# Reordering the work in front of a fused kernel's tile loop, and three small moves inside the loop

## The reference, cut to what matters

```python
# x: (64, 64, 1024), float32; W is L0_ffn_weight (1024, 1024)
y = grouped_conv(x, L0_cond_weight, K=9, groups=4) + (cond_128 @ c_weight.T)[:, :, None] + bias
w_scale = max(abs(W), axis=-1) / 127;  w_q = round(W / w_scale)          # int8, per row
a_scale = max(abs(y), axis=-1) / 127;  y_q = round(y / a_scale)          # int8, per token
x = x + float16((y_q @ w_q.T) * a_scale * w_scale.T)
# second layer, float32
h = gelu(gelu(cond_128 @ W0 + b0) @ W1 + b1);  att = softmax(h @ W2 + b2)
u = einsum('boi,bih->boh', einsum('bk,koi->boi', att, weight), x) + (att @ bias_k)[:, :, None]
H = u @ W2nd.T + b;  z = u @ A
gate = top-2 softmax gate of H[:, odd tokens, :8] and z[:, odd tokens] @ LiMEs.T, scaled by their global maxima
x = x + H + ((z * (gate @ LiMEs)) @ Bmat) * 0.5
```

## Time and profile before

| | |
|---|---|
| median of 3 runs | 624.28 us (623.23 to 624.49) |
| the profiled execution | 624.99 us |
| its span, first to last instruction | 623.2 us |
| PE busy | 612.7 us (98%) |
| DVE, ACT, POOL busy | 423.5, 348.1, 374.2 us |
| mean granted TensorE clock | 0.999 |

### The profile page before, as it was taken

One profiled execution on the slowest core, in us unless ns is written; L12 is line 12 of the kernel. 1 busy time (PEld: TensorE's weight loads), 2 busy tenths in 40 slices (PEclk: granted clock), 3 DMA queues, 4 the chain that ended last, 5 costly groups with the idle time before them and its releaser, 6 DMA issues.

```text
span 623.2 us, 15758 instructions
## 1 busy us (share of the span) xinstructions
PE 612.7 (98%) x6297; PEld 343.4 (55%) x6297; DVE 423.5 (68%) x845; ACT 348.1 (56%) x614; POOL 374.2 (60%) x252
## 2 busy tenths in 40 slices
PE   8999999999999999999999999999999999999997
PEld 6756666666666776666454444444444444444443
DVE  5868888977888888887688976664535444345534
ACT  2878999778988888875652442545153332233000
POOL 3316554547766666546596948798967656865300
PEclk9999999999999999999999999999999999999999
DMA  8968998888888988774056105855455344544203
GB/s 346 334 192 281 390 303 281 277 301 296 309 315 317 317 315 305 267 268 171 38 205 237 35 4 186 321 209 197 168 203 168 137 157 181 170 135 140 101 31 135
DMA packets 38342, 136.21 MB, mean 219 GB/s; under 512 B 5004, under 2 KB 5292, under 8 KB 38225
## 3 DMA queue, kind: packets, MB, share of 16 engines
q1 hardware_dynamic: 33518, 118.43, 54.8%
q10 hardware_dynamic: 4752, 16.78, 6.7%
HBM read 87.95 MB, written 47.24 MB: 217 GB/s over the span
## 4 chain that ended last, share of the span: by engine, by line
PE 78%; DVE 4%; issue 1%; ACT 1%; DVEq 0%; ACTq 0%
PE ps L884 41%; PE ps L611 13%; PE ps L516 7%; PE ps L686 4%; PE ps L649 4%; PE ps L595 4%; PE ps L866 2%; PE ps L580 2%; PE ps L669 1%; PE ps L623 1%; DVE yb L1421 0%; PE ps L619 0%; ACT yv L996 0%; DVE yb L1727 0%; PE ps L654 0%
## 5 line engine op out<-in xcount | busy, mean ns | idle before, releaser
L611 PE MATMUL ps<-wqT,yq_both 128*128 128x512 bf16 x512 | 120.9, 379 | 0.6 <-DVE yb L1421 0.6
L1247 POOL TENSOR_TENSOR x<-x_in,f_all 128x512 f32<-128x512 f32 x64 | 74.0, 1159 | 51.9 <-DVE f_all L1456 51.2
L1251 POOL TENSOR_TENSOR x_split<-x_ph,x_split 128x1032 f16<-128x1032 f32 x25 | 53.7, 2147 | 62.8 <-ACT x_split L969 62.8
L996 ACT ACTIVATE yv<-yb,yinv 128x128 f32<-128x128 f32 x256 | 77.9, 387 | 1.2 <-DVE yinv L1447 1.1
L1286 POOL TENSOR_TENSOR ring<-ring 128x512 f32<-128x512 f32 x56 | 72.8, 1300 | 4.3
L611 PEld LDWEIGHTS ps<-wqT,yq_both 128*128 128x128 bf16 x512 | 45.5, 97 | 47.9 <-issue 1.0
L1456 DVE SCALAR_TENSOR_TENSOR f_all<-ps,tok_scale,wsc_b 128x512 f16<-128x512 f32 x64 | 48.0, 749 | 20.6 <-PE ps L611 19.6
L516 PE MATMUL ps<-x_split,conv_h 128*64 128x256 f16 (+1 forms) x1248 | 59.8, 274 | 0.0
L516 PEld LDWEIGHTS ps<-x_split,conv_h 128*64 128x64 f16 (+1 forms) x1248 | 48.6, 108 | 8.4 <-issue 5.2
L1034 ACT ACTIVATE ring<-ring,pair_inv 128x1024 f32<-128x1024 f32 x28 | 30.6, 1139 | 36.1 <-DVE wst L1765 11.9
L1778 DVE SCALAR_TENSOR_TENSOR x_in<-ps,unscale,x_in 128x512 f32<-128x512 f32 x30 | 22.5, 750 | 40.8 <-PE ps L884 40.7
(11 more groups left out here) (341 smaller groups left out, 1241.8 us busy)
## 6 DMA issues: line engine op xcount, KB each, us to landing
x_in<-in_x SPq DMA_DIRECT2D x32, 512.0 KB, 6.1
x_scratch<-x SPq DMA_DIRECT2D x32, 512.0 KB, 3.4
x_ph<-in_x_phases SPq DMA_DIRECT2D x31, 516.0 KB, 4.8
x_scratch<-ring SPq DMA_DIRECT2D x26, 512.0 KB, 4.9
ring<-x_scratch SPq DMA_DIRECT2D x26, 512.0 KB, 5.3
x_in<-x_scratch SPq DMA_DIRECT2D x12, 512.0 KB, 3.9
out<-x_in ACTq DMA_DIRECT2D x12, 512.0 KB, 2.7
wst<-in_w_rows SPq DMA_DIRECT2D x10, 512.0 KB, 6.7
```

Source lines behind the costliest of these rows:

```text
L611: last = mm(acc_bank(t, h), yqT[:, t % 2, p, :], wqT[:, p, h * HALF:(h + 1) * HALF], start=p == 0, stop=p == PH - 1)
L996: last = A(yv[:, s, :], yb[:, t % 2, s, :], ACT.Copy, scale=yinv[:, s:s + 1], bias=MAGIC)
L1247: g.tensor_tensor(x1[:, t % 2, s], x_in[:, t % 3, s], f16[:, s], ALU.add).then_inc(sem("x1_ready"), 1)
L1251: g.tensor_tensor(x_split[:, (t - SPLIT) % 2, 1, :], phases(t), x_split[:, (t - SPLIT) % 2, 0, :], ALU.subtract).then_inc(sem("xl_ready"), 1)
```

## The change

Six edits; nothing that is computed changes.

1. POOL fills `ones_b` ahead of the identities, and `warm` multiplies `ones_b` with itself spread to 512 columns, as soon as it is there: 11, 2 and 2 products where 28, 6 and 6 of 128 columns stood. The fourth group, `warm(8)`, is gone, and the transposition of W's block 0 takes its place ahead of `conv(0)`.
2. The rest of the work in front of the loop stands in another order on PE, DVE and ACT. `conv(1)` comes ahead of `max_rows(0)`, `conv(2)` ahead of `tokens_out(0)`, `wq_scales_out(0)` and blocks 5 and 6. DVE makes all three steps of a block of W together, and copies the second half of W's scales in ACT's place.
3. In step 13 PE transposes `w_max` behind the convolution and spreads `w_top` behind the first half of the integer product; DVE reduces between `conv_bias` and `row_max` of that step.
4. `w_ends` stays at the top of step 29; `b_ends` moves to the end of step 29. PE waits for `w_ends` alone.
5. The z biases run in steps 5, 8, 11 and 12.
6. SP's and PE's counts of `row_parts_ready` are fitted to this. SP's own order is the same.

The diff, cut to its core (the new order of DVE and ACT in front of the loop is left out where edit 2 says it):

```diff
-                    mm(bank(3)[:, 0:P], identb[:, :], identb[:, :], start=True, stop=True)
-            pe.wait_ge(sem("ident_ready"), 2)
-            warm(28)
+                    mm(bank(3), ones_b[:, :], ones_b[:, :].unsqueeze(1).to_broadcast([P, 4, P]), start=True, stop=True)
+            pe.wait_ge(sem("ones_ready"), 1)
+            warm(11)
...
-            warm(8)
+            wq_transposed(0)
             pe.wait_ge(sem("conv_w_loaded"), 16)
             conv(0)
...
-            wq_transposed(0)
             wq_transposed(1)
             agg_weights(0)
+            conv(1)
+            max_rows(0)
+            wq_transposed(2)
+            agg_weights(1)
+            max_back(0)
+            wq_transposed(3)
...
             wq_transposed(4)
+            pe.wait_ge(sem("yinv_ready"), 1)
+            max_rows(1)
+            conv(2)
+            max_back(1)
             tokens_out(0)
             wq_scales_out(0)
             wq_transposed(5)
             wq_transposed(6)
             int_product(0, 0)
             pe.wait_ge(sem("yinv_ready"), 2)
             max_rows(2)
+            wq_transposed(7)
+            wq_scales_out(1)
             tokens_out(1)
...
+                if c == W_BOUND + 1:
+                    pe.wait_ge(sem("w_max_ready"), 1)
+                    wait(pe, "yinv_ready", c)
+                    tr(ps_small[0:1, 160:288], w_max[:, :], ident[:, :]).then_inc(sem("w_top_psum"), 1)
                 mix(c - 3)
...
                     if c == W_TURN + 2:
-                        pe.wait_ge(sem("row_parts_ready"), 4)
+                        pe.wait_ge(sem("row_parts_ready"), 1)
                     rank_pair(c - 5)
...
-                if 5 <= c < 9:
-                    z_bias(c - 5)
+                if c in (5, 8, 11, 12):
+                    z_bias((5, 8, 11, 12).index(c))
...
+            chan_max(2)
+            dve.wait_ge(sem("wsc_psum"), 2)
+            v.tensor_copy(wsc_b[:, HALF:L], bank(3)).then_inc(sem("wsc_ready"), 1)
...
                 conv_bias(c)
+                if c == W_BOUND + 1:
+                    dve.wait_ge(sem("w_top_psum"), 1)
+                    v.tensor_reduce(w_top[:, :], ps_small[0:1, 160:288], AX.X, ALU.max).then_inc(sem("w_max_ready"), 1)
                 row_max(c)
...
+                if c == W_TURN + 2:
+                    row_parts(b_ends, bias_flat[:, :], s_up[:, 4:5])
```

More of the change, by code:

```diff
@@ L731, in _ @@
             wq_transposed(5)
-            max_rows(1)
             wq_transposed(6)
-            max_back(1)
-            conv(2)
-            wq_transposed(7)
-            wq_scales_out(1)
             int_product(0, 0)
@@ L777, in _ @@
                     pe.wait_ge(sem("s_scale_ready"), 1)
+                if c == W_BOUND + 1:
+                    pe.wait_ge(sem("w_max_ready"), 2)
+                    mm(ps_small[:, 300:301], w_top[:, 0:1].to_broadcast([1, P]), ident[0:1, 0:1], start=True, stop=True).then_inc(sem("w_top_psum"), 1)
                 if SPLIT <= c + LEAD < NT:
@@ L1091, in _ @@
             scale_rows(0)
-            wq_out(3)
             wq_out(4)
             tokens_sb(0)
-            wsc_out(0)
+            act.wait_ge(sem("wsc_psum"), 1)
+            A(wsc_b[:, 0:HALF], bank(2), ACT.Copy).then_inc(sem("wsc_ready"), 1)
             wq_out(5)
@@ L1218, in _ @@
             g = nc.gpsimd
+            g.memset(ones_b[:, :], 1.0).then_inc(sem("ones_ready"), 1)
             g.memset(ident[:, :], 0.0).then_inc(sem("ident_zero"), 1)
@@ L1227, in _ @@
             g.memset(ones16[:, :], 1.0)
-            g.memset(ones_b[:, :], 1.0)
             g.memset(z_w[:, :, :], 0.0).then_inc(sem("zeros_ready"), 1)
@@ L1529, in rank_out, with row_parts @@
                                            z_lo[:, 0:P], ALU.mult, ALU.add).then_inc(sem("z_ready"), 1)
-            def row_ends_b():
-                for o, src, up in ((w_ends, rank_bank(0)[0:NL, 256:256 + P], w_up[0:NL, 0:1]), (b_ends, bias_flat[:, :], s_up[:, 4:5])):
-                    link(v.tensor_scalar(o[:, 0, :], src, up, None, ALU.mult))
-                    v.scalar_tensor_tensor(o[:, 1, :], src, up, o[:, 0, :], ALU.mult, ALU.subtract).then_inc(sem("row_parts_ready"), 2)
+            def row_parts(o, src, up):
+                link(v.tensor_scalar(o[:, 0, :], src, up, None, ALU.mult))
+                v.scalar_tensor_tensor(o[:, 1, :], src, up, o[:, 0, :], ALU.mult, ALU.subtract).then_inc(sem("row_parts_ready"), 1)
             def pair_scales():
@@ L1608, in _ @@
                 if c == W_TURN + 2:
-                    row_ends_b()
+                    row_parts(w_ends, rank_bank(0)[0:NL, 256:256 + P], w_up[0:NL, 0:1])
                 if c >= 6 and c % 2 == 0:
```

86 lines of the change are left out of this document (27 added, 59 removed).

## The result

The changed kernel takes 618.97 us (median of 4 runs, 618.62 to 619.33), the kernel before beside it 624.38 us (median of 4, 623.23 to 624.65). The ratio is 0.9927, with a 95% interval of 0.9908 to 0.9946. The prediction was 617.8 us, in a range of 616.8 to 621.0. The profiled execution of the changed kernel took 619.33 us, with a span of 617.5: 5.7 us less span than the trace of before.

The account below looks back on a forecast made before the run. PE, busy for 612.7 of 623.2 us, was taken to bound the kernel. Gains of 2.9, 1.6, 0.85 and 1.15 sum to 6.5 us, taking the median from 624.28 to 617.8 us, range 616.8 to 621.0.

Parts of the forecast that it names:

- the rival of step 29: Step 29: w_low goes ahead of scale_phases, so conv_bias(29) stays late and nothing is gained there; 619.0 us, chance 0.12.
- Part 1: Front of the loop: new order and early full PE pace start conv(3) at 37.3 instead of 40.36; gain 2.9 us.
- The rival of a late doubling: Front: PE's pace doubles only at about 14 us, front gain 0.8 to 1.2; total 619.8 us, chance 0.2.
- the forecast of 5 to 8: Front: PE reaches full pace from somewhere between 5 and 8 us, after an unbroken stretch of warm-up products.
- the sign named for part 1: Front: 16 products of conv(0) in a microsecond from its start would show the full pace.
- Part 2: Steps 7 and 9: moving z biases off ACT in steps 6 and 7 removes PE's waits; gain 1.6 us.
- the lower end's case: z biases: only step 7 gains, if step 8's bias still delays step 9; 0.8 us.
- Part 3: W's maximum, steps 12 and 13: step 12 gains 0.99, the transposition costs 0.15 in step 13; gain 0.85 us.
- Part 4: Row ends, step 29: b_ends moved to the step's end lets scale_phases start before w_low; gain 1.15 us.
- leftover: Step 29: about 0.2 us of PE's 1.38 us wait expected to remain.
- The rival in which the wait changes hands: Step 29: w_low comes first, scale_phases waits until 268.2, the row ends bring nothing; 619.0 us, chance 0.12.
- a rival's sum: Slower than before: PE's slow pace lasts far into the front; until 27 us it would give 625.7 us, chance 0.03.

Follow-up runs that it names:

- the third comparison: Changed kernel again, with versions lacking warm-up, with b_ends ahead of w_ends, or with three further moves, beside the kernel before: changed 619.40 us, before 623.58, ratio 0.9939.
- part 2 undone: Changed kernel with the z biases back in steps 5, 6, 7 and 8: 620.36 us, ratio 0.9961 to the kernel before.
- the further version: Changed kernel with tile 2's phases issued earlier, three z biases moved later, W's transposition right ahead of step 12's rows' maximum: 617.98 us, ratio 0.992 to the kernel before.

## Why the prediction was right, and where it wasn't

The change moved the profile by 5.7 us, where the sum said 6.5; by the medians it was 5.4 on one chip and 4.2 on another. The measured 618.97 lies in the range, but 0.3 above the narrow band (616.8 to 618.7) that had the chance of 0.55, and just where the rival of step 29 put it (619.0), whose mechanism did not occur: the time alone would have pointed to the wrong cause. Point by point, against the trace of before:

- **Part 1, 2.9 forecast, 2.75 found.** `conv(2)` at 23.88 (23.9), a wait for the copies of W of 0.41 (0.4 to 0.6), `conv(3)` at 37.44 (37.3); `mix(0)` cost 0.17 in the end (0.2). The chain from the landing of the phases was the right one, and it was the limit: a kernel that lets them land earlier gains 0.79 more. The rival of a late doubling fell: it came at 4.1 us here, and at 3.7 to 6.5 in the other traces with this warm-up, around the early end of the forecast of 5 to 8.
- **The reading of the earlier trace rows was faulty.** 8 products, then 16 in the next microsecond, were taken as a doubled pace. But `conv(0)` ends with products of half the rows, which run four at a time where the others run two. PE's windows in the changed kernel's `conv(0)`, full pace throughout (window, length, busy and products, granted clock, DMA share, GB/s), show nearly the same step:

```profile
10.00:11.00 1.00, 1.00 (x10) 1.00 1.02 418
11.70:12.70 1.00, 1.00 (x18) 1.00 1.02 415
```

  So the sign named for part 1, 16 products in a microsecond from the start of `conv(0)`, could not come at any pace. The pace did double there in the trace of before, but what shows it is the duration of one instruction of one form: products of 128x256 took 634 ns up to 13.3 us, and the last two of that form, from 14.1, 380. Ahead of the doubling the clock's column reads 1.00 as well as behind it; it does read 0.50 behind PE's last product, from 621.7 us in that trace.
- **What the prediction didn't ask:** whether the late doubling is in every execution of the kernel before. It isn't. Against a trace with the doubling at 11.1 the front of the changed kernel gains 1.42 us at `conv(3)`, not 2.92. The forecast held the time because the runs shown were close to the profiled one. That was luck: in the third comparison the medians lie 4.2 us apart, where the sum said 6.5.
- **Part 2, 1.6 forecast, 1.23 found.** Step 7 as worked out (0.87). The mis-sized term is step 9: 0.36 instead of 0.71. The prediction held that ACT would have the remaining bias of step 8 in hand; it was the lower end's case, by half, and moving that bias too gave the other 0.35. With part 2 undone, PE waits for ACT not at `tokens_out` alone but at `x_total`, too, which the prediction didn't name.
- **Part 3, 0.85 forecast, 0.53 found.** Step 12 gave its 0.99. The mis-sized term is the cost in step 13, 0.46 instead of 0.15. The transposition between a convolution and a mix costs 0.36, as the further version shows by taking it away, and not the 0.15 read off a transposition that stood among its like. The other 0.10 is the spreading, which the sum left at nothing: behind the first half of the integer product it costs PE more than behind the mix, where it stood before (step 13 takes 9.63 us in the further version and 9.52 with the spreading at its old place).
- **Part 4, 1.15 forecast, 1.39 found.** The order held, `scale_phases` came first by 0.30 us (0.15 forecast) and took 0.90 us, not 1.48, and no leftover remained. The rival in which the wait changes hands fell.
- **Not forecast:** the pause of 0.36 in step 25, and a gain of 0.10 behind the last mark.
- **A slip in a rival's sum:** with the slow pace until 27 us, 12.9 us beyond 14.1 at 0.5 each take 6.45 from the 4.5 of the rest, which gives 626.2 us and not 625.7. The forecast doesn't use it.

The parts sum to 2.75 + 1.23 + 0.53 + 1.39 - 0.36 + 0.10 = 5.64 us, and the spans differ by 5.7. The total was near because the misses were small, three terms down by 0.84 together and one up by 0.24; the pause took another 0.36.

## What to carry to other kernels

Before you cost a late clock, look at a second execution: the moment of the doubling can differ between executions of one kernel, and a single trace charges or credits the change with it. Read the pace from the duration of one form of instruction, never from counts across forms, nor from the granted clock's column ahead of the first doubling. In this kernel a small instruction of VectorE on SBUF data cost the rest of what GpSimd had begun ahead of it, and the next one was caught again, so such work belongs where GpSimd is idle; a small product cost least among small products (0.11 us against 0.36).

## What the runs showed of the hardware

- TensorE's pace in the first microseconds has two levels (it is read as the clock's 1.2 and 2.4 GHz), 631 and 379 ns for 128x512 bf16, 333 and 192 ns for an f32 weight load of 128x128, and in the traces the second did not give way to the first again up to the last product. 28 narrow products from 2.05 us and then a gap brought it at 11.1 us once and at 13.9 once; a stretch without a gap from 0.99 us brought it at 3.7 to 6.5 us in nine traces, one of them with narrow products and one with the old order; one from 2.19 us at 6.4 with wide products and at 13.7 with narrow ones; with no such products it came at 15.8.
- Five untraced executions with a mean granted clock of 0.997 took 1.4 to 2.6 us more than the others of their kernels with 0.999 and 1.000.
- Two operations of VectorE on 128x8 elements in SBUF took 0.96 and 2.05 us beside GpSimd's instructions of 1.16 and 2.13 us, and 0.22 and 0.23 all but without them; two with an operand in PSUM took 0.29 and 0.34 beside the short one. The other way round, `w_low` took 2.60 us instead of 2.13 when a VectorE instruction of 0.90 us had begun 0.30 us ahead of it.
- TensorE paused 0.36 to 0.72 us in the same mix of step 25 in the traces of four kernels (twice for the changed one) and not in others, with nothing that the trace shows it waiting for.
